# Moving one band's convolution in front of two other blocks in TensorE's order (two-layer FFT/convolution block, one core)

## The reference

```python
def layer(x):                                  # x: (4, 32, 128, 128)
    v = group_norm(x, groups=32)               # one channel per group
    xm = einsum('bchw,oc->bohw', v, W_in)      # 32 -> 3 * 85 channels
    s, f, gate = split(xm, 3, axis=1)
    s = depthwise_conv3x3(s, W_dw)             # 85 channels, SAME
    f = irfft2(rfft2(8x8 patches of f) * fft_weight)
    return einsum('bchw,oc->bohw', gelu(gate) * (s + f), W_out)
x = x + layer(x); x = x + layer(x)
```

## Time and profile before

| | us |
|---|---|
| Median of 3 runs | 803.64 (802.22 to 804.83) |
| The profiled execution, device time | 804.34 |
| Its span in the trace | 802.2 |
| Busy: PE / PEld / DVE / ACT / POOL | 729.7 / 622.4 / 542.9 / 564.6 / 646.3 |
| Mean granted TensorE clock | 0.978 of full |

### The profile page before, as it was taken

The page is one execution under the profiler, slowest core; times in us unless marked ns, Lnnn a source line. Parts: engine busy times, 40 slices in busy tenths (PEclk is TensorE's granted clock), DMA queues, the critical chain, the costliest instruction groups (busy, mean ns, idle before and its releaser), DMA issues.

```text
span 802.2 us, 32072 instructions
## 1 busy us (share of the span) xinstructions
PE 729.7 (91%) x12322; PEld 622.4 (78%) x12322; DVE 542.9 (68%) x956; ACT 564.6 (70%) x1087; POOL 646.3 (81%) x1106
## 2 busy tenths in 40 slices
PE   2598799898999889998999999999999999999897
PEld 1487578777888678887888788888888888888785
DVE  7696577768777767667766676667666665666443
ACT  2676477666777767777877677777777777777664
POOL 2986877799877997889888898778797887778771
PEclk9699899999999999999999999999999999999999
DMA  7569566965666646766676667787767777777741
GB/s 297 151 172 252 117 170 171 253 161 135 156 175 166 171 114 155 178 172 177 156 172 161 160 180 185 188 203 197 183 179 192 183 182 191 195 206 182 195 128 54
DMA packets 91041, 140.70 MB, mean 175 GB/s; under 512 B 28514, under 2 KB 31322, under 8 KB 90506
## 3 DMA queue, kind: packets, MB, share of 16 engines
q1 hardware_dynamic: 64006, 110.78, 53.1%
q0 software_dynamic: 26496, 27.61, 14.1%
q10 hardware_dynamic: 388, 0.27, 0.1%
HBM read 10.91 MB, written 8.56 MB: 24 GB/s over the span
## 4 chain that ended last, share of the span: by engine, by line
PE 50%; DVE 12%; issue 11%; SPq 10%; POOL 8%; DMA 5%; ACT 3%; DVEq 0%; ACTq 0%; POOLq 0%
PE ps_s L499 20%; PE ps_ft L554 8%; PE ps_o L565 6%; SPq L295 5%; SPq L301 5%; PE ps_g L505 3%; POOL xs L378 3%; PE ps_s L605 3%; PE ps_s L603 3%; PE ps_z L587 3%; DVE g L1049 3%; DVE xf L997 2%; DVE y L1068 2%; PE ps_x L479 2%; POOL yl L798 2%
## 5 line engine op out<-in xcount | busy, mean ns | idle before, releaser
L499 PE MATMUL ps_s<-cw,stack 128*128 128x85 f16 (+1 forms) x7168 | 449.6, 204 | 11.8 <-DVE g L1049 6.3
L499 PEld LDWEIGHTS ps_s<-cw,stack 128*128 128x128 f16 (+1 forms) x7168 | 370.4, 99 | 39.3 <-DVE g L1049 9.2
L378 POOL DMA_DIRECT2D xs<-xf x757 | 383.8, 512 | 8.6 <-issue 5.0
L798 POOL TENSOR_TENSOR yl<-y,yh 128x340 f16<-128x340 f32 x256 | 221.5, 868 | 112.2 <-ACT yh L726 109.6
L726 ACT ACTIVATE yh<-y 128x340 f16<-128x340 f32 x256 | 124.6, 487 | 159.4 <-PE ps_s L605 100.9
L1068 DVE TENSOR_TENSOR y<-ps_z,weff 128x340 f32<-128x340 f32 x256 | 129.5, 506 | 134.3 <-PE ps_z L587 117.5
L981 DVE TENSOR_TENSOR parts<-xn,parts 128x1024 f16<-128x1024 f32 (+2 forms) x99 | 121.7, 1231 | 69.4 <-ACT parts L656 68.3
L554 PE MATMUL ps_ft<-squares_sb,g 128*85 128x128 f32 x1024 | 164.3, 283 | 1.2 <-ACT turned_results L714 1.2
L719 ACT ACTIVATE g<-ps_g,gsc 128x340 f32<-128x340 f32 x256 | 136.9, 535 | 34.3 <-PE ps_g L505 33.9
L714 ACT ACTIVATE turned_results<-ps_ft 85x512 f32<-85x512 f32 x256 | 148.0, 578 | 15.7 <-PE ps_ft L554 15.6
L1049 DVE TENSOR_TENSOR g<-ps_s,g 128x340 f32<-128x340 f32 x256 | 128.6, 502 | 33.2 <-PE ps_s L605 31.7
(11 more groups left out here) (110 smaller groups left out, 568.3 us busy)
## 6 DMA issues: line engine op xcount, KB each, us to landing
stack<-parts SPq DMA_DIRECT2D x496, 130.0 KB, 3.4
xs<-xf POOLq DMA_DIRECT2D x757, 32.0 KB, 2.5
out_y<-yo SPq DMA_DIRECT2D x16, 512.0 KB, 3.1
stack<-parts SPq DMA_DIRECT2D x124, 65.0 KB, 2.5
stack<-parts SPq DMA_DIRECT2D x124, 64.5 KB, 2.4
stack<-parts SPq DMA_DIRECT2D x124, 64.0 KB, 2.3
x<-in_x SPq DMA_DIRECT2D x3, 2048.0 KB, 10.8
x<-in_x SPq DMA_DIRECT2D x4, 512.0 KB, 5.6
```

The source lines that it names most:

```text
L378: eng.dma_start(xs[C * k:C * k + C, h % HELD, q, :], xf[C * q:C * q + C, h % 2, SPECTRA[k], :]).then_inc(loaded, 16)
L499: mm(ps_s[i % 2][:, HID * q:HID * (q + 1)], pixels(kind, i, q, dy, rows), w[0:rows, m, :], start=(q == 0 and m == 0), stop=False)
L798: nc.gpsimd.tensor_tensor(yl[:, k, :], y32[:, k, :], yh[:, k, :], ALU.subtract).then_inc(s_yl, 1)
```

## The change

In the loop over i, the call that issues band 3's convolution of tile i moves up by two blocks. Instructions, operands, buffers and waits stay as they were; only TensorE's order changes.

```diff
                 if live(i, 0):
                     gate(i, range(Q // 2, Q)).then_inc(s_gate, 1)
                     conv(i, 2)
+                    conv(i, 3)
                 if live(i, 2):
...
                 if i in transforming:
                     transform(transforming[i])
                 if live(i, 0):
-                    conv(i, 3)
                     s, k = ps_s[i % 2], i % 2
                     need(pe, s_yh, i + 1)
                     mm(s[:, 0:GC], inv, yh[:, k, :], start=False, stop=False)
```

## The result

The changed kernel ran in 798.9 us (median of 17 runs, 794.7 to 805.5), the kernel before beside it in 805.5 (17 runs, 799.9 to 810.4): ratio 0.9929, interval 0.9908 to 0.9950. That is 5.7 us less (4.0 to 7.4). The forecast was 3.7 us. The single execution varies by several us, more than the effect. So whole times are taken from the ratios, and the traces are used for what happens at one place.

What follows compares the result with a forecast made beforehand. TensorE, 91% busy, was taken as the bound, gaining only where it idles, chiefly at the transform; 1.4 + 2.0 + 0.3 = 3.7 us off 803.64 gave 799.9, say 800.0; 8-in-10 range 795.5 to 804.8.

Steps and rivals of the forecast that it cites:

- the sum: Whole kernel: 1.4 us from eight strips, 2.0 from seven, 0.3 at the late spectrum; together 3.7 us won.
- The block fills waits at the transform; the later z shifts DVE's row: TensorE before the transform: 0.29 us of work fills waits, but z and the DVE row starting with it come 0.29 later.
- 0.17 a strip in the first layer, 0.29 in the second: Transform at 4 modulo 8: `lo_part`'s wait for ACT absorbs 0.17 us of the shift, in the second layer all 0.29.
- The upper bound: The 35 waits at the transform: all but three are 0.28 or more, so at most 32 x 0.29 = 9.3 us.
- Nothing at 0 modulo 8: Second layer, iterations at 0 modulo 8: few waits, under 0.3 us; their row starts with z without slack, nothing won.
- In the first layer norm moves away from the `yl`: harmless: DVE's norm, first layer: shifts by 0.29, from 409.99 to 410.28, away from POOL's `yl`, without harm.
- the slower rival: First-layer norm falls on POOL's `yl` if that comes over 0.8 us later, in some 14 strips; near 809; chance 0.12.
- The late `yl` costs nothing: Eight waits of the inverse for POOL's `yl`: preceded by POOL's own queue; cost 0, within -0.3 and +2.3 us.
- SP takes the gain back in eleven strips: Strips 0, 14, 16, 18, 19, 22, 23, 25, 26, 27, 29: SP's loads set the length, TensorE's gain is waited off.
- First two strips nothing: Strips 0 and 1: gain lost to SP's loads and to a 1.72 us wait of the inverse for POOL.
- All filled: Rival: all waits at the transform are filled, as DVE's row follows ACT and SP has slack; 795.4 us; chance 0.08.
- Nothing left: Rival: the row moves with z everywhere or late `yh` eats 0.17, and SP catches up; about 803.0 us; chance 0.30.

Runs made afterwards that it cites:

- the order with z in place: Band 3's convolution put between z and the transform, z no later than in the kernel before; against that kernel 0.9894 from six runs, again 0.9891.
- the one with z last: Changed kernel with z moved further back, behind the transform and directly in front of the inverse; 1.0066 against the kernel before.
- SP relieved: Three of each strip's 28 stack loads issued by ACT in place of SP; against the kernel before, old order 0.9925, changed order 0.9836.
- the relieved pair: Old and changed order, both with three of each strip's 28 stack loads on ACT; 0.9925 and 0.9836 against the kernel before.
- the three parts: Band 3 moved only in tiles 0 to 15, 128 to 255, or 16 to 127; against the kernel before 1.0008, 0.9971 and 0.9977.

## Why the prediction was right, step by step

The time, 798.9, lies 1.1 us under the forecast; against the ratio, 5.7 (4.0 to 7.4) was measured for 3.7. Mechanism and sign were right. That the size came out near was in part luck: the sum left out losses and gains of 1 to 2 us each, told in the steps below.

- **The block fills waits at the transform; the later z shifts DVE's row.** Shown: by the rows above (0.29 of shift, 0.17 of slack), by the order with z in place (3.27) and by the one with z last, which is slower than the kernel before.
- **0.17 a strip in the first layer, 0.29 in the second.** The medians have 0.19 and 0.29. The upper bound was miscounted: of the 35 waits all but one are of 0.28 or more, so it is 34 x 0.29 = 9.9, not 9.3; nothing rests on it.
- **Nothing at 0 modulo 8.** This step failed. With SP relieved the median goes from 2.62 to 2.44 in the second layer. Strip by strip the two profiles differ in five of the twelve, by 0.19 to 0.38 us (21, 22, 25, 26 and 29), 1.4 us in all with the small ones; that and thirteen times 0.29 make up 5.2 of the 5.4 us between them. The prediction had seen that norm, moved into the `yl`, would end hardly later, and called that only "mildly good", because the list showed hardly a wait at the transform behind. There was one, too short to stand in the list: such iterations took 2.60 us before where none was listed (strips 21, 25 and 29), and 2.44 is the floor. Norm and `yl` of the changed kernel (compare):

```profile
496.01 1.31 DVE L957 TENSOR_SCALAR xn<-x,mv,rstd 128x1280 f32<-128x1280 f32 x1
```

```profile
495.76 0.85 POOL L798 TENSOR_TENSOR yl<-y,yh 128x340 f16<-128x340 f32 x1
```

  Norm fell from 1.59 to 1.31 us, so hardly any of the 0.29 us of shift reached the row's end, and the block could fill the wait. The first layer has no such gain: strips 3, 4 and 7 take 2.52 at this place in both orders.
- **In the first layer norm moves away from the `yl`: harmless.** True for most strips, wrong for two. At the beginning of strip 14 the norm of the edge column meets a `yl`:

```profile
383.44 1.31 DVE L965 TENSOR_SCALAR xn<-edge,mv,rstd_edge 128x128 f32<-128x128 f32 x1
```

```profile
383.76 0.84 POOL L798 TENSOR_TENSOR yl<-y,yh 128x340 f16<-128x340 f32 x1
```

  It took 0.40 before, and the iteration takes 3.60 us in place of 2.70. At that of strip 11 norm takes 1.37 for 0.94, and the iteration 2.94 for 2.58. Both appear in all four profiles that have the new order in these tiles. Together 1.3 us lost: the slower rival's collision, in two strips and not in fourteen, and not by its condition. It wanted a `yl` later by 0.8 us. Here `yl` kept its place (0.74 us after the inverse's second half before, 0.72 after), and the edge norm moved by its own 0.28 into it. The Trainium skill (SBUF — State Buffer, Who interferes with whom) says that whoever issues first holds the shared ports for its whole length. By recorded starts this is a second counter-example: the edge norm starts 0.32 ahead of `yl`, and is the one that grows. Other runs went by the rule, see the last section.
- **The late `yl` costs nothing ("I take 0").** This step failed too, in two strips. At the beginnings of strips 9 and 13 the inverse waited 1.46 to 1.48 us for `yl` in four profiles of the old order, and the iteration takes 4.6 us in place of 4.3 in all four with the new one. Before, then after:

```profile
270.64 0.32 PE L605 MATMUL ps_s<-yl,waves 128*128 128x340 f16 x1 [1.46 <-POOL yl L798]
```

```profile
266.47 0.32 PE L605 MATMUL ps_s<-yl,waves 128*128 128x340 f16 x1 [1.74 <-POOL yl L798]
```

  In front of this `yl` POOL issues four DMAs of the statistics, three of which take 0.55 to 0.58 us. The one during which DVE's norm ends takes longer, and in both strips of all fourteen profiles it ends 0.11 to 0.13 us after norm does. Norm is in the row that starts with z. It ended at 266.53 before and this issue took 0.83 (from 265.82); after the change norm ended at 262.36 and the issue took 1.12 (from 261.37). So the whole 0.29 came through: a collision of DVE and POOL that the prediction had not looked for, as it read POOL's own queue as something that does not move. With band 3 between z and the transform both iterations take 4.32, as before.
- **SP takes the gain back in eleven strips.** Shown for the second layer, eight of the eleven, by the relieved pair: 5.4 us apart against some 0.8. For strips 0, 14 and 16 it isn't shown; the delay of 0.40 us at strip 15 that the prediction read is 0.14 to 0.15 in two other profiles of the old order. The sum had let 1.5 us of it survive without relief. The traces show 0.8; as the strips' delays vary by several us from one execution to the next, these two do not differ.
- **First two strips nothing.** Not contradicted: 1.0008, and a gain of over 1.7 us is excluded.
- **The sum.** In the traces the stretch from strip 2 to 16 took 335.0, 336.8, 336.3 and 337.5 us in four profiles of the old order, and 332.4, 333.8, 333.2 and 332.6 in four of the new: 3.4 us apart in the mean (2.2 expected for these strips with the late spectrum). But only part of it stands in every profile. At 4 modulo 8 of strips 2 to 15, without 5 and 9, the old order takes 40.2 to 41.2 us and the new one 38.1 to 38.2: 2.6 won. At 0 modulo 8 of strips 9, 11, 13 and 14 the old takes 13.9 and the new 15.7 to 15.8: 1.8 lost. The remaining 2.7 lie in waits that come and go with the execution, such as one iteration of 8.0 us in place of 2.5 in a profile of the old order. So 0.7 us is sure for the first layer, and the second layer's 0.8 is a mean over profiles that differ by 3.4 among themselves. Whether the rest, up to the 5.7 of the ratio, is the change's stays open; the three parts, timed by themselves, sum to 3.6.
- **Rivals.** "All filled" (795.4) is refuted by `lo_part`'s lost slack, and by the order with z in place, which fills more and is about 3 us faster than the change. "Nothing left" is refuted by the ratio.

## What to carry to other kernels

Before moving a block into a wait, walk back from what ends the wait to the last point where its engine was idle; if that point is released by something which the move makes later, only the slack between the two is won. Do the same for every other wait that the row feeds: here a norm that slid onto a `yl` and onto a DMA issue of POOL took back 1.8 us of the 2.6 won in the first layer. Here the block belonged behind the producer (z) and in front of the waiting consumer (the transform): same fill, no delay, 0.989 in place of 0.993. And look at what paces the period as a whole: three of 28 DMA issues moved off SP were worth as much as the change, and took the best order from 0.989 to 0.973.

## What was not expected of the hardware

- A granted clock of 0.79 in the stretch from 62 to 70 us of the kernel before, where TensorE had idled 2.2 us: seven matmuls stood as 0.66 us in place of 0.45. The 0.79 is the mean of a piece at the lower level, 1.2 GHz, behind the idle time, and the rest at 2.4. In the changed kernel's profile the idle time there was 1.46 us, and the clock stayed at 1.00; its own drop came after 4.5 us of waiting at 76.4. Which strip loses the clock differed between these two executions, and is a part of the 3.5 us that looked like an effect.
- A DMA issue of POOL is held up by DVE's norm: it takes 0.55 to 0.58 us alone, and 0.71 to 1.15 where norm ends during it. Its end then lies 0.11 to 0.13 us behind norm's, in 28 cases of 28 (the statistics' DMAs at strips 9 and 13, fourteen profiles, five orders of TensorE).
- DVE's norm (0.94 us alone) takes longer when a `yl` of POOL overlaps it, while `yl` keeps its 0.84: 1.31 when `yl` started 0.25 us before it, 1.59 when it starts 0.04 after it, 1.71 to 1.78 at 0.2 after, 2.01 to 2.04 at nearly 0.5 after. Of 104 norms in the fourteen profiles with a `yl` that starts up to 0.5 us after them, 88 are lengthened so.
- The other 16 are all those of the two kernels with z in front of bands 2 and 3. There `yl` starts 0.30 or 0.31 us after norm, norm keeps its time and `yl` is the one that grows, which is the outcome of the rule cited above. At the same distance, 0.31, the norm of 1152 columns takes 1.78 at 569.26 in the kernel before. So the recorded starts do not decide which engine is held up; what does is not shown here. Second layer, z in front, SP relieved:

```profile
488.79 0.95 DVE L963 TENSOR_SCALAR xn<-x,mv,rstd 128x1280 f32<-128x1280 f32 x1
```

```profile
489.09 1.33 POOL L804 TENSOR_TENSOR yl<-y,yh 128x340 f16<-128x340 f32 x1
```
